# First attention of an eight-stage network: scores from 32 key rows at their own row position, two groups interleaved

## What is computed

```python
x = L0_attn_x                                   # (8, 256, 256)
x = _layernorm(x + _L0_attn_ref(x, wq, wk, wv, wo))
...
def _L0_attn_ref(x, wq, wk, wv, wo):            # QH, KVH, HD = 16, 4, 16
    q = apply_rope(heads(x @ wq, 16))           # (b, 16, 256, 16)
    k = apply_rope(heads(x @ wk, 4))            # (b, 4, 256, 16), each shared by 4 query heads
    v = heads(x @ wv, 4)
    attn = q @ k.T / sqrt(16)                   # (b, 16, 256, 256)
    attn = softmax(where(causal, attn, -inf))
    out = attn @ v
    return out.reshape(b, t, d) @ wo
```

## Time and profile before

| | |
|---|---|
| time, median of 3 runs | 3296.48 us |
| the three runs | 3294.09, 3298.33, 3296.48 us |
| span of the profiled execution | 3294.2 us |
| PE busy | 2885.3 us (88%) |
| DVE, ACT busy | 1903.6 us (58%), 1284.9 us (39%) |
| the stage changed | about 17 to 352 us of the span |

### The profile page before, as it was taken

The page is one execution under the profiler, slowest core; times in us unless marked ns, Lnnn a source line. Parts: engine busy times, 40 slices in busy tenths (PEclk is TensorE's granted clock), DMA queues, the critical chain, the costliest instruction groups (busy, mean ns, idle before and its releaser), DMA issues. The chain is left out here.

```text
span 3294.2 us, 44074 instructions
## 1 busy us (share of the span) xinstructions
PE 2885.3 (88%) x14664; PEld 2204.1 (67%) x14672; DVE 1903.6 (58%) x4499; ACT 1284.9 (39%) x3325; POOL 127.8 (4%) x96
## 2 busy tenths in 40 slices
PE   7999699989999999999598877798778886799997
PEld 6888544446777767777476665547666665678776
DVE  3555533334454554545645857647777775677777
ACT  2222155544344443443222132208666774223232
POOL 0000000000000000000022000001111110000000
PEclk8999799999999999999799988899888887799998
DMA  3000200000000000000200000100000001000000
GB/s 146 6 6 3 103 1 0 0 0 7 3 0 3 3 3 3 0 3 0 86 0 0 0 1 0 40 1 32 16 13 16 16 10 78 38 1 0 0 0 25
DMA packets 25115, 54.76 MB, mean 17 GB/s; under 512 B 3552, under 2 KB 21728, under 8 KB 23392
## 3 DMA queue, kind: packets, MB, share of 16 engines
q1 hardware_dynamic: 25056, 54.02, 4.4%
HBM read 39.33 MB, written 2.10 MB: 13 GB/s over the span
## 5 line engine op out<-in xcount | busy, mean ns | idle before, releaser
L1592 PE MATMUL psum<-l3a_kr,l3a_qr 128*128 128x128 f32 (+1 forms) x1024 | 271.3, 395 | 7.0 <-ACT l3a_pr L1697 3.7
L1697 ACT ACTIVATE l3a_pr<-psum,l3a_nm 128x128 f32<-128x128 f32 (+1 forms) x512 | 207.2, 431 | 167.0 <-DVE l3a_nm L1796 166.8
L108 DVE TENSOR_TENSOR x_sb<-psum,x_sb 128x512 f32 (+2 forms) x48 | 41.7, 869 | 317.6 <-PE psum L845 135.5
L1592 PEld LDWEIGHTS psum<-l3a_kr,l3a_qr 128*128 128x128 f32 x1024 | 179.6, 218 | 42.0 <-issue 17.0
L1796 DVE TENSOR_REDUCE l3a_nm<-psum 128x2 f32<-128x256 f32 (+1 forms) x256 | 130.1, 550 | 92.0 <-PE psum L1594 90.8
L363 ACT ACTIVATE l0a_pr<-psum,l0a_nm 128x128 f32<-128x128 f32 (+1 forms) x256 | 86.6, 421 | 235.9 <-DVE l0a_nm L417 235.9
L656 DVE TENSOR_TENSOR l0f_hg<-l0f_sq,psum 128x512 f32<-128x512 f32 x128 | 87.7, 687 | 156.0 <-ACT l0f_sq L598 152.2
L2009 PE MATMUL psum<-l3f_x_hi,l3f_w_hi 128*128 x384 | 154.5, 402 | 7.2 <-DVE l3f_w_lo L2092 7.2
L890 ACT ACTIVATE l1a_pr<-psum,l1a_nb,l1a_rq 128x128 f32<-128x128 f32 (+1 forms) x256 | 127.2, 509 | 85.0 <-DVE l1a_nb L943 85.0
L2010 PE MATMUL psum<-xT,l3f_w_hi 128*128 x384 | 152.8, 398 | 0.0
L2011 PE MATMUL psum<-l3f_x_hi,l3f_w_lo 128*128 x384 | 152.1, 396 | 0.0
(11 more groups left out here) (420 smaller groups left out, 7172.2 us busy)
## 6 DMA issues: line engine op xcount, KB each, us to landing
w_l3f_all<-l3f_all_dram SPq DMA_DIRECT2D x1, 9216.0 KB, 25.8
l3a_qr<-l3a_q_all SPq DMA_DIRECT2D x32, 256.0 KB, 2.5
w_l0f_w<-l0f_w_dram SPq DMA_DIRECT2D x2, 2048.0 KB, 9.8
w_l1f_all<-l1f_all_dram SPq DMA_DIRECT2D x1, 2560.0 KB, 8.8
x_sb<-x_dram SPq DMA_DIRECT2D x1, 2048.0 KB, 8.4
l0a_xc<-xT SPq DMA_DIRECT2D x8, 256.0 KB, 2.5
w_l1a_q<-l1a_q_dram SPq DMA_DIRECT2D x1, 2048.0 KB, 8.1
w_l1a_k<-l1a_k_dram SPq DMA_DIRECT2D x1, 2048.0 KB, 12.6
```

The lines of the kernel that those rows point to most:

```text
L1592: mm(S[n % 2][:, a, t * P:t * P + (t + 1) * P], qr[:, a, r, t * P:(t + 1) * P], kr[:, g, a, 0:(t + 1) * P], start=True, stop=False)
L1697: last = nc.scalar.activation(pr[:, m % 2, a, j, s], S[j][:, a, s], ACT.Exp, bias=nm[:, j, t, a:a + 1], accum_out=sums[:, m % 2, a, j, t:t ...
```

## The change

The keys lose their planes: `kr` is one tile of 128 rows with the four groups' keys in their 32 rows each, written by one addition instead of four, and without zeros. The score product takes only the 32 rows of its group, from both operands, and is placed at that row position of the array (`tile_position=(32 * g, 0)`). The order within `scores` changes: the four score products come first, the two groups taken in turn for each t, and the four mask products behind them. Since a bank's two score products now come before any mask, only the first has `start=True`.

```diff
-        kr = sb("kr", [P, G, T])
+        kr = sb("kr", [P, T])
...
-                    for i in range(2):
-                        r, g = n // 2, n % 2 * 2 + i
-                        for t in range(TT):
-                            dst = S[n % 2][:, i, t * P:t * P + (t + 1) * P]
-                            mm(dst, qr[:, r, t * P:(t + 1) * P], kr[:, g, 0:(t + 1) * P], start=True, stop=False)
+                    r = n // 2
+                    for t in range(TT):
+                        for i in range(2):
+                            g = n % 2 * 2 + i
+                            rows = slice(32 * g, 32 * g + 32)
+                            mm(S[n % 2][:, i, t * P:t * P + (t + 1) * P], qr[rows, r, t * P:(t + 1) * P], kr[rows, 0:(t + 1) * P],
+                               start=(t == 0), stop=False, tile_position=(32 * g, 0))
+                    for t in range(TT):
+                        for i in range(2):
                             last = mm(S[n % 2][:, i, 2 * t * P:(2 * t + 1) * P], c["idb"], c["maskb"],
-                                      start=False, stop=True)
+                                      start=False, stop=(t == TT - 1))
...
-                nc.vector.memset(kr[:, :, :], 0.0).then_inc(rot_steps, 1)
...
-                    dve.wait_ge(rot_steps, b + 2)
-                    for g in range(G):
-                        rows = slice(32 * g, 32 * g + 32)
-                        last = nc.vector.tensor_tensor(kr[rows, g, :], k1[rows, 0, :], k1[rows, 1, :], ALU.add)
-                    last.then_inc(rot_ready, 1)
+                    dve.wait_ge(rot_steps, b + 1)
+                    nc.vector.tensor_tensor(kr[:, :], k1[:, 0, :], k1[:, 1, :], ALU.add).then_inc(rot_ready, 1)
```

## The result

| | before | changed |
|---|---|---|
| median | 3295.28 us | 3366.06 us |
| ratio, 95% interval | | 1.021 [1.0196, 1.0225] |
| span of the profiled execution | 3294.2 us | 3356.9 us |

A forecast was written before the change was run, and what follows sets the result against it. The stage was taken as bound by PE; 42 `scores` savings of 0.23 us (9.7) plus 1.3 for the keys' addition made 11.0, span 3294.2 to 3283.2, and 2.3 more for the median gave 3285.5 us; range 3274 to 3332.

The forecast's parts named there:

- The step that failed: Slower rival on PE's clock: 32-row score products hold it less, so PE falls to 0.50 between projections; chance 0.13.
- The sum behind 3285.5 us: Whole kernel: 9.7 us from shorter `scores` plus 1.3 from the keys' addition, 11.0 us saved.
- the same clock drops as before: Sign of a right forecast: PE's granted clock drops as often as before, give or take two.
- The rival's size: Clock rival: up to 190 us lost between projections, less 11, giving 3475 us; half if it falls half the time.
- The eight passes: Float32 score passes in one `scores`: 0.88, 1.19 or 1.30 us, by how far the two groups overlap.
- the lower bound: The eight score passes at full overlap, each group's second pass beside the next group's first: 0.88 us.
- Drains, loads and masks: Rest of one `scores`: 0.10 entering 32 rows, 0.11 load, 0.11 returning to 128, 0.17 masks; sum 0.49 us.
- the other slower rival: Every change of group in `scores` drains like a change of size: 33 us slower, 3329 us; chance 0.10.
- Where savings vanish: At a change of batch element, three of eight `scores` savings are lost to waits for ACT's and DVE's copies.
- The count of 42 savings: Of 64 `scores` savings, 35 in batch elements 2 to 8 and 7 in the first reach the end; 9.7 us.
- The keys' addition: One addition instead of four saves 1.28 us, uncovered only at the start's 1.68 us wait: 1.3 us back.
- the first case: Groups overlap in `scores`: saving 4 to 17 us, 3285.5 us, own range 3275 to 3294; chance 0.60.

The follow-up runs named there:

- e2: The changed kernel with score products of 64 rows instead of 32, keys in two planes with zeros and four key additions kept; 3281.41 us, ratio 0.9962.
- e11: The 64-row kernel e2 without the score products of the second of a pair's two heads, so half the scores are missing; 3366.09 us, ratio 1.0232.
- e3: The 128-row reordered kernel e1 without the score products of the second of a pair's two heads; 3271.72 us, ratio 0.9933.
- e4: The changed kernel with four added 128-row products of zeros in each scores block; 3312.32 us, ratio 1.0056.
- e7: The changed kernel with eight added 128-row products of zeros in each scores block; 3291.83 us, ratio 0.9998.
- e1: The kernel before with only the changed order: 128-row score products first, groups in turn, then the four masks; 3292.13 us, ratio 0.9996.
- e5: The 64-row kernel e2 with the next batch element's three projections parted and put between values and turns; 3274.53 us, ratio 0.9941.
- e9: e5 with DVE's layer norm statistics moved behind the next batch element's first copies of transposes; 3255.87 us, ratio 0.9880.

## Why the prediction was wrong

1. **The step that failed** is in the rivals: "If a 32-row product holds the clock less than a 128-row one, PE falls to 0.50 between projections". It had a chance of 0.13, on the ground that "nothing shows that rows count". It is what happened. The sum behind 3285.5 us priced every duration at the full clock and expected "the same clock drops as before", so it put the clock's cost at nothing; it was 112 us by (1 - clock) x length. With the same products, order and overlap, 32 rows against 64 (changed, e2) is 85 us. With the same matmuls on 64 instead of 128 rows (e11, e3) it is 94 us, 89 of them by the clock. With the other half of the array empty (e11, e2) it is 85 us. Full-height products of zeros give the time back by steps (e4, e7).
2. **The rival's size** was 190 us, or half of that if the clock is down half the time, less the saving of 11. The clock was down in two thirds of the stage (0.67 is 66% at 0.50) and cost 112 us more than before, of which the shorter blocks gave back 40. A period at the half clock is only 2.07 us longer than one before (5.77 against 3.70), not doubled, because the block had become shorter.
3. **The eight passes** are the term that was mis-sized: said to lie between 0.88 and 1.30 us, they took 0.65. I let the second pass of one product block the first of the next, in program order. In fact both passes of one group run beside both of the other, and leaving one group out saves nothing (0.85 us in e11 as in e2). The block saves 0.61 us, not 0.23, and the lower bound was no bound. The direction of this term was right.
4. **Drains, loads and masks** were right: a first load of 0.11, a drain of 0.09 and passes of 0.65 make 0.85 against the measured 0.86, and e1's period is 0.16 shorter against 0.17 expected. That every change of group drains, the other slower rival, is ruled out by two loads within 0.01 us.
5. **Where savings vanish** was right in part. PE stood 6.7 to 7.9 us before the second turns with shorter blocks (changed, e2, e5), 1.2 at most in one element, and e9 removed just that wait. The wait for ACT's copy was there where the clock was high, 4.2 us in e2 and 3.0 in e5. In the changed kernel it was not, 0.7 us once where over 1.0 was forecast for each element. The count of 42 savings fits e2: 11 us, and 14 that the clock took, against 42 x 0.61 = 26. It does not fit the changed kernel, where 40 us were saved, as much as all 64 blocks and the keys would give (64 x 0.61 + 1.3); at the half clock the other engines have more time to be ready. That last point is argued from these sums and was not tried.
6. **The keys' addition** was right: the wait at the start fell from 1.68 to 0.4 us. The first score product starts 2.3 us earlier; 1.3 of it are the keys, and the rest is a clock drop that lay there before and is gone in this execution.
7. **Slips in the working** move nothing. By their own terms the passes' bounds are 0.87 and 1.20, not 0.88 and 1.19, and the range of the first case reaches to 3296 (3292 and 4), not 3294. The rival of drains at each change of group would pass 6.6 us from 0.045 us for each change on (57 x (3 x 0.045 + 0.04) - 3.3), not from 0.015. By the difference of the two loads' 206 and 104 ns the short load occupies 0.01, not 0.02.

The Trainium skill, page "TensorE: Matmul & The Clock Gate", Part 3, has products in different row groups start 4 ns apart with loads overlapping. The rows agree (two loads and two matmuls that start within 0.01 us), and they add that this holds for float32 products of two passes.

## What to carry to other kernels

When a change makes products use fewer rows of the array, first ask what holds the clock in that stretch: here the full-height score products did, and taking them away cost more than the overlap gave. Two halves of 64 rows side by side gave the same overlap as two of 32 and kept all 128 rows in use; padding with zeros, which looks like waste, was what paid. Then look where the faster engine arrives too early: at the full clock the sums fit with five of eight savings reaching the end, and a reordering on DVE took away the wait of 7.9 us that held two of the others.

## What the runs showed of the hardware

- The granted clock of this stage depends on the rows in use. PE was busy 97% of the stage in the changed kernel and had a clock of 0.67; with the same loads and columns on 64 rows it was 0.89 (e2), and with e2's second half left empty 0.70 (e11). Rows and columns of zeros count: the added rows of e2 and the added products of e4 and e7 (0.82, 0.91) add only zeros.
- The same steady work can run at either clock for long: 17 us at 1.00 and 17 us at 0.50 in one execution. In both batch elements the clock rose to 1.00 within about 1 us of the end of the output projection; one held it through those 17 us, the other lost it after some 7 us. What decides between them was not tried.
- Two float32 products of different row positions and PSUM banks, loads included, run side by side in full: 0.65 us where the passes one after another add up to 1.30, and as long as one group's alone (e11).
- A change between 128 rows and 32 or 64 costs about 0.09 us of drain and an exposed load. The loads' idle time before the masks, in which the last passes and this drain lie, reads 0.33 at the full clock and 0.65 at the half, so both scale with the clock.
- Adding 512 matmuls to a kernel in which PE sets the pace left it 74 us faster (e7 against the changed kernel).
